# A two-layer graph network on one core: GpSimd copies ahead of each indirect DMA, a rebuilt placing stage, and fp32 query and value tables

## The chip, the core and the metric

The kernel runs on one core of a Trainium2 chip. A core has TensorE (PE, with its weight loads PEld), VectorE (DVE), ScalarE (ACT), GpSimd (POOL), a sync engine (SP) that issues plain DMAs, on-chip SBUF and PSUM, and 16 DMA engines. The metric is device time in microseconds (us) of one execution. Each engine works through its own queue in order; semaphores tie the queues together.

## What is computed

There are N = 6250 nodes with 128 features (NW = 49 windows of up to 128 rows), and E = 100000 edges, each with a source and a destination, sorted by destination in the input. Cut to what matters:

```python
# layer 0: attention over edges, H = 8 heads of D = 16
q = (x @ Wq.T + bq).reshape(N, H, D);  k, v alike
scores = sum(q[src] * k[dst], -1) / sqrt(D) + mask          # E x H
weights = softmax of scores over the edges of one src
out = segment_sum(v[src] * weights, dst) ; x = layernorm(x + out @ Wo.T + bo)
# layer 1: edge network
h = silu(concat(x[src], x[dst], attr) @ eW1 + eb1)
e = silu(h @ eW2 + eb2) ; agg = segment_sum(e, src)
x = layernorm(x + silu(concat(x, agg) @ nW1 + nb1) @ nW2 + nb2)
```

## The kernel before

The kernel is written with a queue for each engine and hand-placed semaphores; nothing reorders it. Its stages follow one another with a barrier between them. Edges are handled in tiles of 128, one edge a partition. The edges are first sorted by source: each edge gets a slot such that a tile of 128 slots holds only edges whose sources lie in one window of 128 nodes. There are 784 input tiles and 832 slot tiles (NT). Four stages issue indirect DMAs from GpSimd, one DMA for a tile of 128 rows, so 128 indices each:

- **Placing** (`place_and_project`), 98 groups of PG = 8 tiles. For each group DVE writes one-hots of the node in the window (`place_oh`) and of the window (`place_ohw`), PE transposes the first (`turn`, L588), forms which edges of a tile share a node (`gram`, L596), keeps a running table of the next free slot (`count`, L607 brings the old table into PSUM as fp32, L610 adds the counts, 400 down to 50 columns), and reads each edge's slot out (`slots_of`, L622 in fp32 and L623 in bf16). ACT copies the table (L541) and two copies of the transpose (L549, L550). DVE masks, reduces and turns the slot into a row number (`finish`, L483 to L521) and copies the 8 tiles' records into `rec_out` (L519). POOL then issues 8 indirect DMAs that scatter 64-byte records to DRAM (`send`, L646). In every second group PE also projects one window of x to q, k, v (L580 bias, L581 product). ACT copies q and v out, and DVE splits each into three bf16 parts (L470, L475) and stores these in the tables `tab` and `value_tab` (L480, L481).
- **Scores** (`score`), 104 groups of SG = 8 tiles. POOL gathers 512-byte rows of k by destination (L751); the index tile `sc_idx` is written by DVE (L761) three groups ahead. PE transposes one-hots (L843) and picks query rows with three bf16 products a tile, one for each part of the table (L853). DVE multiplies (L779) and reduces.
- **Weighing** (`weigh`), 208 groups of 4 tiles: values picked in three bf16 products (L1202), weighted, edges of one destination merged in a tile (L1212), and scattered with an add into one of four sums in DRAM (L1060). Every one of these DMAs has a semaphore wait and increment of its own ahead of it (L1058, L1059).
- **Edge network** (`edges`), 208 groups of 4 tiles: POOL gathers 512-byte rows (L1685) with indices that DVE writes (L1694); PE does transposes, `inputs` (L1790 to L1795), `second` (L1806) and `sums` (L1816); ACT turns and applies silu (L1749, L1755, L1760); DVE makes one-hots, widens them (L1707) and adds sums (L1716).

The gathers have a ring of RING = 4 buffers. In the score stage the queue of GpSimd holds, for a group, one wait on the index and one on the buffer, then 8 DMAs with nothing between them; in the edge network 4 DMAs. `c.tab` holds 3 x NP bf16 values a partition, where NP = 6272.

## Time and profile before

| what | value |
|---|---|
| median of 3 runs | 6206.48 us (6205.77 to 6213.38) |
| profiled execution: its own time | 6212.46 us |
| its span, first to last instruction | 6210.7 us |
| busy share of the span: PE, POOL, DVE, ACT | 64%, 59%, 36%, 18% |
| DMA moved | 238.36 MB, 38 GB/s on average |
| mean granted TensorE clock | 0.709 of 2.4 GHz |

How to read it. The share of an engine over the whole span hides the stages: each has its own limit. A group row of the profile gives the busy time of all its instructions, the mean duration of one, and the idle time just ahead of them, with what ended it: a named instruction (a semaphore that it posted), "issue" (nothing that the profile shows), or "remote" (the engine was released by a semaphore for which the profile finds no post at that moment). A timeline row gives start and duration in us of one instruction or of several merged ones (xN).

### The profile page before, as it was taken

The numbers are of one execution on the slowest core, as the hardware profiler recorded it, in microseconds if no ns is written. First come the engines' busy times: TensorE is split into PE (matmuls) and PEld (weight loads), VectorE is DVE, ScalarE is ACT, GpSimd is POOL, SyncE is SP. The second block draws the span as 40 slices with busy tenths as digits, with TensorE's granted clock in tenths as the row PEclk, the third lists the DMA queues.
The fourth block names the chain that finished last, engine by engine and source line by source line (L and its number), as shares of the span: only waits on it lengthen the run. The fifth ranks groups of instructions, "written<-read, shape, count | busy, mean of one in ns | idle before, by whom it ended". The sixth has DMA issues, their size and how long they took to land. (4 is left out here: it accounts for less than half of the span.)

```text
span 6210.7 us, 91570 instructions
## 1 busy us (share of the span) xinstructions
PE 3972.2 (64%) x25409; PEld 3165.9 (51%) x25410; DVE 2244.2 (36%) x6257; ACT 1098.0 (18%) x1914; POOL 3674.3 (59%) x3321
## 2 busy tenths in 40 slices
PE   6899999994333443430666666666445887777786
PEld 4556656663222222220555555555424777777774
DVE  6334444442222222329333333333244333333333
ACT  0222222220101111110111111111111222222222
POOL 0465555555666666650888888888702565555551
PEclk9996555555555565565777777777657888888888
DMA  2100000001111111110443434443341111111111
GB/s 102 68 10 10 10 9 10 10 10 62 42 44 44 42 43 43 42 40 0 36 36 35 35 35 35 35 35 35 33 126 40 40 42 40 41 40 41 41 40 53
DMA packets 278673, 238.36 MB, mean 38 GB/s; under 512 B 57254, under 2 KB 246758, under 8 KB 278245
## 3 DMA queue, kind: packets, MB, share of 16 engines
q0 software_dynamic: 198144, 170.19, 17.7%
q1 hardware_dynamic: 77604, 54.50, 2.8%
q10 hardware_dynamic: 2880, 13.11, 0.5%
q8 instruction: 24, 0.39, 0.0%
q14 instruction: 21, 0.17, 0.0%
HBM read 143.89 MB, written 93.71 MB: 38 GB/s over the span
## 5 line engine op out<-in xcount | busy, mean ns | idle before, releaser
L1060 POOL DMA_INDIRECT sums_dram<-we_merged_rows,we_idx x832 | 1287.0, 1547 | 425.7 <-issue 200.7
L1685 POOL DMA_INDIRECT ed_bg<-b_rows_dram,ed_idx x832 | 801.2, 963 | 550.6 <-issue 246.3
L652 POOL DMA_INDIRECT records_dram<-rec_out,row_idx x784 | 769.0, 981 | 568.1 <-DVE rec_out L519 331.4
L751 POOL DMA_INDIRECT sc_k<-k_rows_dram,sc_idx x832 | 800.5, 962 | 463.5 <-issue 250.3
L1212 PE MATMUL ps_merged<-we_rows,we_same_dst 128*128 128x129 f32 x1664 | 357.0, 381 | 584.7 <-issue 435.7
L853 PE MATMUL ps_q<-tab,sc_oht 128*128 x2496 | 366.6, 261 | 403.7 <-issue 398.5
L1212 PEld LDWEIGHTS ps_merged<-we_rows,we_same_dst 128*128 128x128 f32 x1664 | 305.6, 274 | 619.3 <-issue 609.3
L1816 PE MATMUL ps_ed_s<-ed_ohf,ed_efs 128*128 128x128 f32 x1664 | 427.4, 413 | 178.5 <-ACT ed_efs L1760 140.7
L853 PEld LDWEIGHTS ps_q<-tab,sc_oht 128*128 128x128 bf16 x2496 | 248.8, 104 | 522.8 <-issue 469.3
L779 DVE TENSOR_TENSOR sc_prods<-ps_q,sc_k 128x1024 f32<-128x1024 f32 x104 | 127.2, 1223 | 915.2 <-remote 862.5
L1816 PEld LDWEIGHTS ps_ed_s<-ed_ohf,ed_efs 128*128 128x128 f32 x1664 | 336.5, 227 | 222.8 <-issue 183.7
L1113 DVE SCALAR_TENSOR_TENSOR we_firsts<-we_merged_rows,lane_unmark,two_marks 128x4 f32<-128x4 f32 x208 | 46.3, 222 | 1014.8 <-ACT we_merged_rows L1156 1014.8
L622 PE MATMUL ps_slots<-place_table,place_oh_tf 128*128 128x50 f32 x1568 | 408.4, 410 | 0.0
L459 DVE TENSOR_TENSOR place_earlier<-ps_gram,tri 128x512 bf16<-128x512 f32 x196 | 126.2, 686 | 763.0 <-PE ps_gram L596 414.4
L622 PEld LDWEIGHTS ps_slots<-place_table,place_oh_tf 128*128 128x128 f32 x1568 | 401.3, 330 | 0.6 <-issue 0.6
L1191 PE MATMUL ps_dst_row<-ident,we_dsts 128*128 128x128 f32 x1664 | 352.8, 384 | 0.0
L1707 DVE CAST ed_ohf<-ed_oh 128x512 f32<-128x512 bf16 x208 | 93.1, 448 | 717.2 <-PE ps_ed_s L1816 443.6
L1156 ACT ACTIVATE we_merged_rows<-ps_merged 128x516 f32<-128x516 f32 x208 | 125.0, 601 | 1280.9 <-DMA sums_dram<-we_merged_rows,we_idx 1266.8
L843 PE MATMUL ps_oht<-identb,sc_oh 128*128 128x128 bf16 x832 | 101.7, 283 | 371.6 <-ACT sc_oht L816 203.3
L1191 PEld LDWEIGHTS ps_dst_row<-ident,we_dsts 128*128 128x128 f32 x1664 | 337.7, 300 | 0.0
L610 PE MATMUL ps_table<-place_ohw,place_oh 128*128 128x400 bf16 (+7 forms) x784 | 332.4, 581 | 0.0
L1792 PE MATMUL ps_z<-ed_oht,tab 128*128 128x128 bf16 x2496 | 302.8, 226 | 40.6 <-issue 39.0
(286 smaller groups left out, 7575.2 us busy)
## 6 DMA issues: line engine op xcount, KB each, us to landing
sc_k<-k_rows_dram,sc_idx POOLq DMA_INDIRECT x832
sums_dram<-we_merged_rows,we_idx POOLq DMA_INDIRECT x832
ed_bg<-b_rows_dram,ed_idx POOLq DMA_INDIRECT x832
sums_dram<-zero_rows ACTq DMA_DIRECT2D x20, 640.0 KB, 8.5
records_dram<-rec_out,row_idx POOLq DMA_INDIRECT x784
co_rows<-sums_dram SPq DMA_DIRECT2D x48, 256.0 KB, 3.9
records_dram<-rfill SPq DMA_DIRECT2D x16, 416.0 KB, 6.9
records<-records_dram SPq DMA_DIRECT2D x1, 6656.0 KB, 18.6
```

The costliest lines, as they stand in the source:

```text
L610: ins = pe.matmul(table[:, k + 1:PG + 1, :], ohl[:, b, :, k], ohw[:, b, :, k].unsqueeze(1).to_broadcast([P, PG - k, WC]), start=False, sto ...
L622: pe.matmul(slots[b][:, k, :], ltf[:, b, k, :], kept[:, b, k, :], start=True, stop=False)
L652: pool.indirect_dma_start(c.rec_rows, bass.IndirectOffsetOnAxis(ap=idx[:, b, j:j + 1], axis=0), out[:, b, j, :], None, bounds_check=SLOTS ...
L751: pool.indirect_dma_start(kg[:, r, k * F:(k + 1) * F], None, c.k_dram[:, :], bass.IndirectOffsetOnAxis(ap=idx[:, r, k:k + 1], axis=0)).the ...
L779: dve.tensor_tensor(prod[:, :], psq[r % 2][:, :], kg[:, r, :], ALU.mult).then_inc(s_prod, 1)
L853: ins = pe.matmul(psq[b][:, k * F:(k + 1) * F], oht[:, b, k, :], c.tab[:, j, bass.ds(win[k] * F, F)], start=(j == 0), stop=(j == 2))
L1060: pool.indirect_dma_start(c.acc_dram[k][:, :], bass.IndirectOffsetOnAxis(ap=idx[:, r, k:k + 1], axis=0), rows[:, r, k, 0:F], None, compute ...
L1191: ins = pe.matmul(psd[:, k * P:(k + 1) * P], dst[:, r, k:k + 1].to_broadcast([P, P]), c.ident[:, :], start=True, stop=True)
L1212: ins = pe.matmul(merged[b][:, k, 0:F + 1], same[:, b, k, :], con[:, b, k, :], start=True, stop=True)
L1685: pool.indirect_dma_start(bg[:, r, k * F:(k + 1) * F], None, c.b_dram[:, :], bass.IndirectOffsetOnAxis(ap=idx[:, r, k:k + 1], axis=0)).the ...
L1792: pe.matmul(z, c.tab[:, j, bass.ds(win[k] * F, F)], oht[:, b, k, :], start=False, stop=False)
L1816: ins = pe.matmul(pss[b][:, k * P:(k + 1) * P], ef[:, b, k, :], ohf[:, b, :, k], start=True, stop=True)
```

## The change

- **Copies ahead of each DMA.** In the score stage and in the edge network GpSimd itself now writes the index tile, by one copy of a 128x1 column a tile (`index`), for the group ahead, one copy in front of each gather. Each gather has a wait on the count of these copies and a semaphore increment of its own. DVE's index casts (L761, L1694) are gone. In placing, GpSimd copies each tile's 128x16 record into `rec_out`, one copy ahead of its DMA, where DVE copied 8 tiles at once (L519). The scatter of the weighing stage is as before.
- **Placing rebuilt.** The one-hot of the window is laid out tile by tile (contiguous in the product), the old table is added by DVE (`keep`, which also splits the new table in two bf16 parts) and no longer by PE and ACT, `slots_of` is three bf16 products a tile, and ACT copies the transpose once. The window's one-hot is written inside `finish`. PE's order in a step is now count, gram, slots. The bias product is bf16, with three parts of the bias in three rows.
- **Tables in fp32.** ACT writes q and v straight into two fp32 tables; the parts and their splitting on DVE are gone. In scores and weighing a tile takes one fp32 product where it took three bf16 ones.

```diff
+def blocks_onehot(dve, c, e, t0, out):
+    return dve.tensor_tensor(out, c.iotab[:, 0:WC, 0].unsqueeze(1).to_broadcast([P, PG, WC]),
+                             e.hi[:, bass.ds(t0, PG)].unsqueeze(2).to_broadcast([P, PG, WC]), ALU.is_equal)
...
+                def keep(i, b):
+                    g = 2 * i + b
                     wait_count(dve, s_slots, g - 1)
+                    dve.wait_ge(s_hist, g + 1)
+                    wait_count(dve, s_tab, 2 * g)
+                    before = e.start[:, :] if isinstance(g, int) and g == 0 else kept[:, 1 - b, PG, :]
+                    dve.tensor_copy(kept[:, b, 0, :], before).then_inc(s_tab, 1)
+                    dve.tensor_tensor(kept[:, b, 1:PG + 1, :], pstab[:, 0:PG * WC].rearrange("p (k w) -> p k w", w=WC),
+                                      before.unsqueeze(1).to_broadcast([P, PG, WC]), ALU.add).then_inc(s_tab, 1)
+                    dve.wait_ge(s_tab, 2 * g + 2)
+                    dve.tensor_copy(kb[:, b, 0], kept[:, b, 0:PG, :]).then_inc(s_parts, 1)
+                    dve.wait_ge(s_parts, 2 * g + 1)
+                    dve.tensor_tensor(kb[:, b, 1], kept[:, b, 0:PG, :], kb[:, b, 0], ALU.subtract).then_inc(s_parts, 1)
...
-                    for by, work in ((1, earlier), (2, nodes), (0, finish), (2, windows)):
+                    for by, work in ((2, nodes), (1, keep), (1, earlier), (0, finish)):
...
-                    act.activation(lt[:, :, :].rearrange("p k n -> p (k n)"), pst[:, :], ACT.Copy).then_inc(s_lt, 1)
-                    act.activation(ltf[:, b].rearrange("p k n -> p (k n)"), pst[:, :], ACT.Copy).then_inc(s_lt, 1)
+                    act.activation(lt[:, b].rearrange("p k n -> p (k n)"), pst[:, :], ACT.Copy).then_inc(s_lt, 1)
...
+                    cols = bass.ds(win * F, F)
+                    act.activation(c.qtab[:, cols], psx[:, 0:F], ACT.Copy, scale=0.25)
+                    act.activation(c.vtab[:, cols], psx[:, 2 * F:3 * F], ACT.Copy).then_inc(s_qv, 1)
...
-                    pe.matmul(psx[:, 0:3 * F], one[:, :], bias[:, :], start=True, stop=False)
+                    pe.matmul(psx[:, 0:3 * F], c.ones[:, :], bk[:, :], start=True, stop=False)
...
-                        pe.matmul(slots[b][:, k, :], ltf[:, b, k, :], kept[:, b, k, :], start=True, stop=False)
-                        ins = pe.matmul(slots[b][:, k, :], gm[:, b, k, :], ohw[:, b, :, k], start=False, stop=True)
+                        for j in range(2):
+                            pe.matmul(slots[b][:, k, :], lt[:, b, k, :], kb[:, b, j, k, :], start=(j == 0), stop=False)
+                        ins = pe.matmul(slots[b][:, k, :], gm[:, b, k, :], ohw[:, b, k, :], start=False, stop=True)
...
+                def record(g, b, j):
+                    pool.tensor_copy(out[:, b, j, :], e.rec[:, bass.ds(g * PG + j, 1), :].rearrange("p t r -> p (t r)")
+                                     ).then_inc(s_rec, 1)
 
                 def send(i, b):
                     g = 2 * i + b
-                    pool.wait_ge(s_rec, g + 1)
+                    wait_count(pool, s_sent[b], 16 * PG * i)
+                    record(g, b, 0)
                     pool.wait_ge(s_idx, g + 1)
-                    pool.sem_inc(s_turn, 1)
                     for j in range(PG):
+                        if j + 1 < PG:
+                            record(g, b, j + 1)
+                        pool.wait_ge(s_rec, PG * g + j + 1)
+                        pool.sem_inc(s_turn, 1)
                         pool.indirect_dma_start(
...
+                def index(g, r, k):
+                    pool.tensor_copy(idx[:, r, k:k + 1], c.rec[:, bass.ds(g * SG + k, 1), C_DST]).then_inc(s_idx, 1)
+
                 def gather(g, r):
-                    pool.wait_ge(s_idx, g + 1)
                     wait_count(pool, s_prod, g - RING + 1)
-                    pool.sem_inc(s_turn, 1)
+                    ahead, slot, there = group_at(g, r, 1, NS)
+                    if there:
+                        wait_count(pool, s_k[slot], (ahead - slot) * (16 * SG // RING))
                     for k in range(SG):
+                        if there:
+                            index(ahead, slot, k)
+                        pool.wait_ge(s_idx, SG * g + k + 1)
+                        pool.sem_inc(s_turn, 1)
                         pool.indirect_dma_start(kg[:, r, k * F:(k + 1) * F], None, c.k_dram[:, :],
...
-                        for j in range(3):
-                            ins = pe.matmul(psq[b][:, k * F:(k + 1) * F], oht[:, b, k, :],
-                                            c.tab[:, j, bass.ds(win[k] * F, F)], start=(j == 0), stop=(j == 2))
+                        ins = pe.matmul(psq[b][:, k * F:(k + 1) * F], oht[:, b, k, :],
+                                        c.qtab[:, bass.ds(win[k] * F, F)], start=True, stop=True)
```

The gather of the edge network is changed as the one of the score stage, with G = 4 in the place of SG, and the value product of the weighing stage as the query product.

How the queues move. First POOL in the loop of the score stage (`sc_k` is the ring of gathered rows, `sc_index`, `sc_prod` and `sc_k_in1` are semaphores; ISA and REGISTER_ALU rows are address and count arithmetic). Before:

```order
L88 REGISTER_ALU [waits sc_index]
L751 DMA sc_k<-k_rows_dram,sc_idx 128x128 [waits sc_prod]
L751 DMA sc_k<-k_rows_dram,sc_idx 128x128 x7
L747 REGISTER_ALU
L88 REGISTER_ALU [waits sc_index]
```

and after:

```order
L88 REGISTER_ALU [waits sc_prod]
L750 ISA [waits sc_k_in1]
L750 COPY sc_idx<-records 128x1
L760 ISA
L762 DMA sc_k<-k_rows_dram,sc_idx 128x128 [waits sc_index]
L750 ISA
L750 COPY sc_idx<-records 128x1
```

Eight DMAs in a row have become eight pairs of a copy and a DMA, and the wait on DVE's index has become one on POOL's own copies.

Then POOL in the loop of placing. Before:

```order
L239 ISA
L652 DMA records_dram<-rec_out,row_idx 106496x16 [waits rec_slot,row_index]
L652 DMA records_dram<-rec_out,row_idx 106496x16 x7
L648 REGISTER_ALU
L652 DMA records_dram<-rec_out,row_idx 106496x16 [waits rec_slot,row_index]
```

and after:

```order
L642 ISA [waits records_sent1]
L642 COPY rec_out<-records 128x16
L649 REGISTER_ALU
L642 ISA [waits row_index]
L642 COPY rec_out<-records 128x16
L655 DMA records_dram<-rec_out,row_idx 106496x16 [waits rec_slot]
```

The wait on DVE's copy of the records (`rec_slot`) is now one on POOL's own, and only the row index still comes from DVE.

Last, PE in placing (`ps_table` is the running table of slots, `place_oh_tf` and `place_oh_t` the fp32 and bf16 transposes). Before:

```order
L623 MATMUL ps_slots<-place_ohw,place_earlier 128x50
L622 MATMUL ps_slots<-place_table,place_oh_tf 128x50
L623 MATMUL ps_slots<-place_ohw,place_earlier 128x50
L607 MATMUL ps_table<-place_table,ident 128x450 [waits place_table_kept,place_onehot_w]
L610 MATMUL ps_table<-place_ohw,place_oh 128x400
```

and after:

```order
L606 MATMUL ps_table<-place_ohw,place_oh 128x100
L606 MATMUL ps_table<-place_ohw,place_oh 128x50
L595 MATMUL ps_gram<-place_oh_t 128x128 [waits place_earlier,place_onehot_t]
L595 MATMUL ps_gram<-place_oh_t 128x128 x7
L618 MATMUL ps_slots<-place_table_parts,place_oh_t 128x50 [waits masked,place_parts,place_earlier]
L618 MATMUL ps_slots<-place_table_parts,place_oh_t 128x50
L619 MATMUL ps_slots<-place_ohw,place_earlier 128x50
```

The 450-column fp32 product is gone, the fp32 product of each tile has become two bf16 ones, and slots now stand behind count and gram.

## Rows read from the trace of the kernel before

**Rows 1.** Busy time of each engine in the four stretches with indirect DMAs.
```profile
core 0: us, PE busy (x) PEld busy (x) DVE busy (x) ACT busy (x) POOL busy (x), PEclk, DMA share, GB/s
190.00:1481.00 1291.00, 1174.12 (x4999) 769.58 (x4998) 526.65 (x1695) 266.42 (x431) 768.56 (x784) 0.63 0.05 10
1513.00:2776.00 1263.00, 488.13 (x3401) 341.91 (x3401) 342.10 (x609) 136.36 (x249) 800.44 (x832) 0.59 0.18 43
2948.00:4489.00 1541.00, 927.08 (x6630) 883.36 (x6630) 500.94 (x1742) 232.92 (x461) 1286.95 (x832) 0.74 0.40 35
4751.00:6093.00 1342.00, 1062.18 (x8555) 949.40 (x8554) 439.51 (x1627) 359.24 (x614) 800.86 (x832) 0.86 0.17 41
```

**Rows 2.** Groups of GpSimd instructions: busy us, mean ns | idle us before, releasers.
```profile
L1060 POOL DMA_INDIRECT sums_dram<-we_merged_rows,we_idx x832 | 1287.0, 1547 | 425.7 <-issue 200.7 <-DVE we_idx L1126 176.8 <-DMA sums_dram<-we_merged_rows,we_idx 47.6
L1685 POOL DMA_INDIRECT ed_bg<-b_rows_dram,ed_idx x832 | 801.2, 963 | 550.6 <-issue 246.3 <-remote 195.3 <-PE ps_z L1795 78.6
L751 POOL DMA_INDIRECT sc_k<-k_rows_dram,sc_idx x832 | 800.5, 962 | 463.5 <-issue 250.3 <-DVE sc_idx L761 213.2
L652 POOL DMA_INDIRECT records_dram<-rec_out,row_idx x784 | 769.0, 981 | 568.1 <-DVE rec_out L519 331.4 <-issue 236.7
```

**Rows 3.** Timeline of GpSimd in the score stage: start, duration, [idle before].
```profile
2013.19 0.94 POOL L751 DMA_INDIRECT sc_k<-k_rows_dram,sc_idx  x1 [0.30 <-issue]
2014.44 0.95 POOL L751 DMA_INDIRECT sc_k<-k_rows_dram,sc_idx  x1 [0.30 <-issue]
2022.75 0.95 POOL L751 DMA_INDIRECT sc_k<-k_rows_dram,sc_idx  x1 [7.36 <-DVE sc_idx L761]
```

**Rows 4.** Timeline of PE and ACT in the score stage, up to the same pause.
```profile
1980.01 3.16 PE L853 MATMUL ps_q<-tab,sc_oht 128*128 x24
1983.17 0.68 PE L843 MATMUL ps_oht<-identb,sc_oh 128*128 128x128 bf16 x8
...
1993.72 0.27 PE L853 MATMUL ps_q<-tab,sc_oht 128*128 x1 [1.13 <-issue]
...
2019.67 1.02 ACT L816 ACTIVATE sc_oht<-ps_oht 128x1024 bf16<-128x1024 bf16 x1 [38.55 <-remote]
```

**Rows 5.** Timeline in the edge network around one pause of GpSimd.
```profile
5220.86 0.94 POOL L1685 DMA_INDIRECT ed_bg<-b_rows_dram,ed_idx  x1 [0.30 <-issue]
5221.97 0.60 ACT L1760 ACTIVATE ed_efs<-ps_ed_o 128x512 f32<-128x512 f32 x1 [8.52 <-remote]
...
5224.38 0.94 POOL L1685 DMA_INDIRECT ed_bg<-b_rows_dram,ed_idx  x1 [2.57 <-remote]
```

**Rows 6.** Waits (us, times, longest): score stage, edge network (two), weighing stage.
```profile
DVE sc_prods L779 <- remote: 862.5, 60, 29.4
...
ACT ed_efs L1760 <- remote: 352.2, 43, 10.1
ACT ed_hts L1755 <- remote: 312.8, 90, 11.5
...
ACT we_merged_rows L1156 <- DMA sums_dram<-we_merged_rows,we_idx: 1266.8, 202, 6.9
```

**Rows 7.** Timeline of GpSimd in the weighing stage.
```profile
3602.14 1.54 POOL L1060 DMA_INDIRECT sums_dram<-we_merged_rows,we_idx  x1 [0.30 <-issue]
```

**Rows 8.** Timeline of placing: GpSimd's pause and PE in one group.
```profile
814.72 0.97 POOL L652 DMA_INDIRECT records_dram<-rec_out,row_idx  x1 [4.50 <-DVE rec_out L519]
815.43 1.83 PE L607 MATMUL ps_table<-place_table,ident 128*128 128x450 f32 x2
...
817.05 3.39 PE L610 MATMUL ps_table<-place_ohw,place_oh 128*128 128x400 bf16 x8
...
820.26 1.03 PE L596 MATMUL ps_gram<-place_oh_t 128*128 128x128 bf16 x8
```

**Rows 9.** Small GpSimd instructions at the program's start: timeline.
```profile
0.35 0.10 POOL L1987 MEMSET const-float32-1.0<- 128x1 f32 x1
0.39 0.10 POOL L1987 MEMSET const-bfloat16-1.0<- 128x1 bf16 x1
...
1.93 0.19 POOL L122 CAST lane_float<-lane_int 128x1 f32<-128x1 int32 x1
```

**Rows 10.** Timeline of the edge network: unstrided fp32 products, four tiles.
```profile
5204.19 1.05 PE L1806 MATMUL ps_ed_o<-w,ed_hts 128*128 128x128 f32 x8
```

160 lines of the change are left out of this document (70 added, 90 removed).

## The prediction

> **What bounds the kernel now.** I read the busy times of four stretches first, then GpSimd's groups, then timelines. The four stages with indirect DMAs fill 5437 of the 6210.7 us [rows 1]; what lies between them (softmax, collecting, normalising) is untouched. For each stage the question is what sets the pace of a DMA.
>
> Placing takes 1291 us for 784 DMAs, 1.65 us each. PE is busy for 1174.12 us of it, POOL for 768.56 [rows 1]. POOL pauses between groups, and what ends the pause is DVE's record copy [rows 8], 331.4 us in total [rows 2]. So placing is bound by PE, and by DVE behind it.
>
> The score stage takes 1263 us for 832 gathers, 1.52 us each. PE is busy for 39%, DVE for 27%, POOL for 63% [rows 1]. A gather is 0.95 us and the next starts 0.30 us later [rows 3], so GpSimd alone would need 832 x 1.25 = 1040 us. The rest is 213.2 us of waiting for DVE's index [rows 2]. But DVE is not busy then. It waits 862.5 us for "remote" [rows 6]. The timelines show something odd: after a run of gathers PE, which did 24 products in 3.16 us, gives out single products with idle gaps of over a microsecond and no wait in them, and ACT's copy of transposes that PE finished by 1983.9 starts at 2019.67 [rows 4]. That is after the gather of 2014.44 was over and GpSimd had nothing more to issue [rows 3]. The edge network has it too: a gather ends at 5221.80, and ACT's silu, after 8.52 us of "remote", starts at 5221.97 [rows 5]. ACT sits 665 us behind "remote" there [rows 6] and GpSimd itself 195.3 us [rows 2]. I read this so: while GpSimd issues gathers back to back, semaphores and instructions of the others come late; when it pauses they catch up, and it pauses only because their lateness reaches it. The edge network takes 1342 us, 6.45 us a group, where PE has 1062.18 / 208 = 5.1 us of work and GpSimd 4 x 1.25 = 5.0.
>
> The weighing stage is the contrast. GpSimd's DMAs stand 0.30 us apart there too, at 1.54 us each [rows 7], but each has a wait of its own ahead of it. ACT's idle time there is put down to landing DMAs, 1266.8 us [rows 6], which is real dependence. This stage is bound by GpSimd.
>
> **The change part by part.** Call c what a copy adds to the period of a DMA. All three stages then hang on it, since I expect each to be bound by GpSimd.
>
> *The copy.* No row shows a copy beside an indirect DMA. From below: two memsets of one column start 0.04 us apart [rows 9], so c is at least about 0.05. From above: a one-column cast takes 0.19 us [rows 9], and if the 0.30 us of handing over [rows 3] were paid a second time, c would be 0.49. The handing over stands ahead of DMAs; small instructions show none of that size between them. I take the cast's duration, c = 0.19.
>
> *Score stage.* The index no longer comes from DVE; the wait on the buffer (`sc_prod`) asks for a product one group older than the old index did, and the wait on the ring's old gathers is long met. If the copies let the others run, the stage is 832 x (1.25 + 0.19) = 1198 us, 65 less. One fp32 product replaces three bf16 ones: 1.05 / 4 = 0.26 us a tile [rows 10] against 3.16 / 8 = 0.40 [rows 4], from different clocks; even at double the first, 0.52, a group's PE work would be some 6 us of the 11.5 that GpSimd takes. Nothing gained or lost.
>
> *Edge network.* GpSimd needs 4 x 1.44 = 5.76 us a group against PE's 5.1, so 832 x 1.44 = 1198 us, 144 less than 1342. PE would be 89% busy and each lateness would show; I add 10 us.
>
> *Placing, PE.* The 450-column fp32 product goes (1.83 us [rows 8], 1.6 of it on PE's path). The counts cost at most the 3.39 us of now [rows 8], less if contiguous one-hots read faster. Slots are 24 bf16 products; at the 1.03 / 8 = 0.13 us of the gram [rows 8] they take 3.1. With gram and turn at 1.0 to 1.1 each and half a projection at 1.2 (its bias product in one pass), the sum is at most 9.8 us a group.
>
> *Placing, DVE.* It is busy for 526.65 / 98 = 5.4 us a group [rows 1]. The splitting and the record copy leave, about 1.2; `keep` comes, four instructions of up to 400 columns, at most 2.5. That gives at most 6.7 us, and the two engines overlap, since PE counts and makes slots for one group while DVE finishes another. What is late next is GpSimd: 8 x (1.28 + 0.19) = 11.8 us. Its period of 1.28 is 0.981 of duration [rows 2] and 0.30 of gap. Placing: 784 x 1.47 = 1151 us, 140 less. The bias parts (eight instructions of 384 columns on DVE ahead of the first projection) cost 5 us once.
>
> *Weighing.* Its scatters are unchanged, and PE has 614 us of slack [rows 1] for the fp32 value product. Nothing.
>
> *The sum.* -140 - 65 - 144 + 15 = -334 us. The profiled span becomes 5877 us. The profiled execution took 6212.46 us, 1.8 over its span and 6.0 over the median, so the median becomes 5877 + 1.8 - 6.0 = about **5875 us**. The gain is gone at c = 0.19 + 334 / 2448 = 0.33 us.
>
> **A rule that speaks against it.** In these stages DVE is busy for 1308 of 3896 us, 34% [rows 1]. The gathers of now hardly feel it: their mean is 962 ns [rows 2] and single ones take 940 to 950 [rows 3].
> The Trainium skill (SBUF — State Buffer, "Who interferes with whom" and the port rules ahead of it) says that VectorE and GpSimd share a pair of ports as an exclusive lock, for VectorE's fast modes and, against a GpSimd instruction that reads SBUF, for those with two SBUF inputs. By that rule the copies, which move from DVE's queue to GpSimd's, would now queue behind DVE; by the rows on the gathers the lock costs little.
>
> **The rivals.**
> *The others stay starved* (the change does not do what it seems made for). The pauses then remain and the copies come on top. For it: a wait every four DMAs in the edge network does not help now, and the weighing stage differs from the gathers in more than its waits, being slower and of the other direction. Against it: in the edge network the release comes 0.17 us after GpSimd falls still [rows 5], so a short stretch without descriptors may be enough. Price: +158 in the score stage, +158 in the edge network, -140 in placing, together +176, about 6380 us. It decides if copies open no gap for the others.
> *The handing over is paid twice*, c = 0.49: 1388 + 1448 + 1448 = 4284 against 3896, so about 6590 us, slower. It decides from c = 0.33. For it: every DMA in the trace has 0.30 ahead of it. Against it: that gap is no longer in the weighing stage, where two more queue entries stand between DMAs [rows 7].
> *The copy is nearly free*, c = 0.05: placing 1041, scores 1082, and the edge network then at PE's pace, some 5.3 us a group or 1102. That is 671 less, with the 15 added about 5550 us. For it: the memsets, and the chance that the copy hides in the 0.30.
> *Copies held up by DVE*: a third of them meeting a DVE instruction and waiting half of some 0.4 us gives 2448 x 0.34 x 0.2 = 166 us, about 6040 us. The skill's rule on the shared ports is the mechanism.
>
> **How the numbers follow.** The forecast with c between 0.10 and 0.28 has 0.46 (5650 to 6090 by itself), the nearly free copy 0.16, DVE's hold-up 0.07, starvation that stays 0.18, the double handing over 0.13. About 0.2% is what a measurement of this kernel can tell from no change. Faster by more: 0.46 + 0.16 + 0.07 less 0.02 for the edge of the forecast, 0.67; slower 0.13 + 0.18 less 0.01, 0.30; within it 0.03. The range leaves out the double handing over and less than half of the free copy: 5560 to 6430 us.
>
> **What would show it.** Right: GpSimd's copies near 0.19 us, DMAs 1.44 to 1.47 us apart without long pauses in all three stages, "remote" waits of ACT and DVE mostly gone, placing's PE well under 80% busy. Starvation stays: "remote" again in hundreds of us and pauses of 5 us and more in the score stage. Double handing over: 0.30 us both ahead of and behind each copy. Wrong in another way: placing still with pauses that a row index of DVE ends, which would make the rebuilt chain through `keep` the bound.

## The result, and the profile after

The changed kernel took 6101.7 us (6088.9 to 6106.9, 4 runs) against 6209.2 us (6205.8 to 6213.4, 4 runs) of the kernel before, measured together: a ratio of 0.983, 95% interval 0.981 to 0.984. That is 108 us less, where 334 less was forecast. Its profiled execution has a span of 6095.8 us.

Busy time of each engine in the four stretches of the changed kernel, as in [rows 1]:

```profile
core 0: us, PE busy (x) PEld busy (x) DVE busy (x) ACT busy (x) POOL busy (x), PEclk, DMA share, GB/s
183.00:1353.00 1170.00, 499.75 (x4755) 384.63 (x4752) 624.72 (x1637) 126.22 (x239) 962.63 (x1566) 0.59 0.05 11
1386.00:2632.00 1246.00, 441.13 (x2572) 379.18 (x2572) 337.04 (x509) 137.73 (x253) 980.70 (x1655) 0.60 0.16 44
2801.00:4341.00 1540.00, 920.82 (x5810) 879.26 (x5810) 499.55 (x1742) 232.92 (x461) 1286.18 (x832) 0.79 0.39 35
4604.00:5981.00 1377.00, 1096.88 (x8589) 967.57 (x8590) 421.30 (x1435) 364.88 (x614) 991.18 (x1660) 0.85 0.15 40
```

Placing fell from 1291 to 1170 us, and PE is busy for 43% of it, no longer 91%. The score stage fell by 17 us only, the weighing not at all, and the edge network grew by 35 us.

GpSimd's groups, to set beside [rows 2] (busy us, mean ns | idle us before, releasers):

```profile
L1701 POOL DMA_INDIRECT ed_bg<-b_rows_dram,ed_idx x832 | 808.3, 972 | 196.7 <-issue 119.9 <-POOL ed_idx L1689 76.9
L762 POOL DMA_INDIRECT sc_k<-k_rows_dram,sc_idx x832 | 804.2, 967 | 152.5 <-issue 132.4 <-POOL sc_idx L750 20.0
L655 POOL DMA_INDIRECT records_dram<-rec_out,row_idx x784 | 776.5, 990 | 206.4 <-issue 108.2 <-POOL rec_out L642 98.2
L642 POOL COPY rec_out<-records 128x16 f32 (+1 forms) x784 | 190.2, 253 | 151.1 <-POOLq L289 112.2 <-DVE row_idx L508 38.2
L1689 POOL CAST ed_idx<-records 128x1 int32 (+1 forms) x832 | 184.8, 222 | 188.4 <-PE ps_z L1809 101.8 <-remote 84.5
L750 POOL CAST sc_idx<-records 128x1 int32 (+1 forms) x832 | 179.7, 217 | 112.4 <-DVE sc_prods L789 109.1
```

In the score stage and the edge network GpSimd no longer waits for an index of DVE. It waits instead for the buffer that DVE's product (`sc_prods`) or PE's product (`ps_z`) frees: 112 us in the score stage and 188 us in the edge network, of which 84.5 are put down to remote. The longest of these pauses in the score stage is 5.8 us. Its timeline in the score stage, beside [rows 3]:

```profile
1998.17 0.96 POOL L762 DMA_INDIRECT sc_k<-k_rows_dram,sc_idx  x1 [0.16 <-issue]
1999.14 0.19 POOL L750 CAST sc_idx<-records 128x1 int32 x1
1999.49 0.96 POOL L762 DMA_INDIRECT sc_k<-k_rows_dram,sc_idx  x1 [0.16 <-issue]
```

A gather starts 1.32 us after the one before, where it was 1.25: the copy takes 0.19 us, but of the 0.30 us of handing over only 0.16 is left behind it. What PE does meanwhile, beside [rows 4]:

```profile
2022.61 0.37 PE L862 MATMUL ps_q<-tab,sc_oht 128*128 x1 [1.73 <-issue]
2024.71 0.37 PE L862 MATMUL ps_q<-tab,sc_oht 128*128 x1 [1.73 <-issue]
2026.81 0.37 PE L862 MATMUL ps_q<-tab,sc_oht 128*128 x1 [1.73 <-issue]
```

The single products with idle time ahead and no wait in them are still there, here 2.10 us apart. In the score stages of both kernels such products start about 0.7, 1.4, 2.1 or 2.8 us apart, most often 0.7, 1.4 or 2.1, though GpSimd's gathers start 1.25 us apart in one and 1.32 in the other. The remote waits are still there too, beside [rows 6]; the one in placing (`place_oh_t`) is new:

```profile
DVE sc_prods L789 <- remote: 821.2, 49, 32.4
...
ACT place_oh_t L552 <- remote: 558.9, 59, 18.4
...
ACT ed_efs L1774 <- remote: 348.1, 55, 10.2
```

Waits of this size need not cost anything: placing has 558.9 us of them on ScalarE, and GpSimd, which sets its pace, has one wait for another engine in it, of 38.2 us (the L642 row above).

One thing has to be known before the experiments are read. Kernels measured together ran on one chip, one after the other; I call that a job. In some jobs the others' work comes late as above, and in other jobs never. I call them late and prompt. Within a job the times of one kernel agree to a fraction of a per cent, so a job is one or the other. The measurement that the prediction was about was a late job.

### The profile page after: what moved, and what is told of

It is laid out like the page before. It is cut to its first block and busy times, and to the rows that moved or that the text cites. A ratio compares the mean times of both kernels' runs of the same rounds, so it can differ in the third digit from the quotient of the medians.

```text
span 6095.8 us, 90649 instructions
## 1 busy us (share of the span) xinstructions
PE 3277.9 (54%) x23500; PEld 2834.4 (46%) x23501; DVE 2316.0 (38%) x5904; ACT 960.4 (16%) x1718; POOL 4241.2 (70%) x5768
## 5 line engine op out<-in xcount | busy, mean ns | idle before, releaser
L1220 PE MATMUL ps_merged<-we_rows,we_same_dst 128*128 128x129 f32 x1664 | 335.4, 364 | 589.9 <-issue 436.7
L1220 PEld LDWEIGHTS ps_merged<-we_rows,we_same_dst 128*128 128x128 f32 x1664 | 286.5, 259 | 625.4 <-issue 616.1
L862 PE MATMUL ps_q<-tab,sc_oht 128*128 x1664 | 341.5, 358 | 219.9 <-issue 206.0
L862 PEld LDWEIGHTS ps_q<-tab,sc_oht 128*128 128x128 f32 x1664 | 294.8, 260 | 249.2 <-issue 248.9
L853 PEld LDWEIGHTS ps_oht<-identb,sc_oh 128*128 128x128 bf16 x832 | 79.8, 159 | 672.7 <-issue 515.2
L606 PE MATMUL ps_table<-place_ohw,place_oh 128*128 128x400 bf16 (+7 forms) x784 | 161.7, 382 | 379.9 <-DVE place_ohw L229 217.4
L1200 PE MATMUL ps_dst_row<-ident,we_dsts 128*128 128x128 f32 x1664 | 328.2, 364 | 0.0
L1689 POOL CAST ed_idx<-records 128x1 int32 (+1 forms) x832 | 184.8, 222 | 188.4 <-PE ps_z L1809 101.8
L606 PEld LDWEIGHTS ps_table<-place_ohw,place_oh 128*128 128x128 bf16 x784 | 111.4, 162 | 436.0 <-issue 378.3
L1200 PEld LDWEIGHTS ps_dst_row<-ident,we_dsts 128*128 128x128 f32 x1664 | 314.0, 281 | 0.0
```

What stands on the lines that cost most here:

```text
L606: ins = pe.matmul(table[:, k:PG, :], ohl[:, b, :, k], ohw[:, b, k, :].unsqueeze(1).to_broadcast([P, PG - k, WC]), start=(k == 0), stop=Tru ...
L853: ins = pe.transpose(pst[:, k * P:(k + 1) * P], oh[:, r % 2, :, k], c.identb[:, :])
L862: ins = pe.matmul(psq[b][:, k * F:(k + 1) * F], oht[:, b, k, :], c.qtab[:, bass.ds(win[k] * F, F)], start=True, stop=True)
L1200: ins = pe.matmul(psd[:, k * P:(k + 1) * P], dst[:, r, k:k + 1].to_broadcast([P, P]), c.ident[:, :], start=True, stop=True)
L1220: ins = pe.matmul(merged[b][:, k, 0:F + 1], same[:, b, k, :], con[:, b, k, :], start=True, stop=True)
L1689: pool.tensor_copy(idx[:, r, k:k + 1], c.rec[:, bass.ds(g * G + k, 1), C_DST]).then_inc(s_idx, 1)
```

## The experiments

Stage times below are from the first to the last start of the stage's indirect DMAs, and a period is the median distance of two starts.

### Parts of the change, one by one

Index copies back to VectorE (placing and tables stay changed):

```diff
+                    pool.wait_ge(s_idx, g + 1)
...
-                        if there:
-                            index(ahead, slot, k)
-                        pool.wait_ge(s_idx, SG * g + k + 1)
```

> The changed kernel, but in the two gathers the index copies are VectorE's again, one for a group, as in the kernel before; placing keeps its GpSimd copies, queries and values their fp32 tables. Theory A: a copy lengthens a gather's period by the 0.064 to 0.071 us that the changed kernel shows, and takes away only part of the pauses, because these come from the others being served late while GpSimd issues gathers back to back; so score returns to about 1263 us (+18) and the edge network to about 1342 us (-34), and the whole is about 6086 us, within 0.5% of the changed kernel. Theory B: the copies are what held the pauses down, and what the changed kernel gained in the score stage is theirs; then score and edge network both grow, by 70 us together or more, 6170 us or more.

Measured: 5572.5 us, but the kernel before took 5702.7 us beside it, not 6209; ratio 0.977 (0.975 to 0.979). Both theories had priced it for a kernel before of 6209 us, so neither could be judged from the absolute time. This job was prompt. The two gather stages took 1048 and 1057 us.

The records of placing by VectorE too:

```diff
+                    dve.tensor_copy(out[:, b, :, :], e.rec[:, bass.ds(g * PG, PG), :]).then_inc(s_rec, 1)
...
-                            record(g, b, j + 1)
```

> As the run before, and the records of placing are copied by VectorE too, one copy for a group of 8 (behind the row index): GpSimd issues DMAs alone, as in the kernel before, but placing keeps its rebuilt counting and slots and its lighter TensorE. Theory A: a placing that GpSimd paces at 1.28 us a scatter takes 784 x 1.28 = 1003 us, plus what it waits for VectorE; if the others are starved there as in the score stage of the kernel before (222 us of pauses in 832 gathers), it takes some 1200 us. So placing lies between 1003 and 1210 us against 1169 us; theory A says pauses ended by VectorE's records or row index of 100 to 200 us in all, and the whole between 6000 and 6120 us. Rival (the shared port): the 115 us that the copies cost beyond 0.067 each in placing come from VectorE and GpSimd holding each other up; without copies placing then falls under 1070 us and the whole under 5990 us.

Measured: 5464.2 us, 0.958 (0.957 to 0.960). Placing is 1060 us, against 1164 us with the eight GpSimd copies. That lies in theory A's range and under the rival's 1070 us as well, and both had reckoned with a late job, so it does not decide between them.

The kernel before with the index copies alone:

> The kernel before with one part of the change alone: GpSimd copies the index in front of each gather, in the score stage and the edge network. Placing, tables and products are those of before. Theory A (starving has nothing to do with how many products TensorE has to fetch): score as in the changed kernel, 1245 us (-17 against before), edge network 1376 us (+34), the whole about 6226 us, +0.3%. Rival (TensorE's 24 products a group in place of 8 are what comes late): score stays at or above 1263 + 54 = 1317 us, since each period grows by 0.064 and no pause goes; the whole 6270 to 6300 us.

Measured: 5838.7 us, 1.024 (1.022 to 1.026). So where nothing comes late, the index copies by themselves cost 136 us, 0.08 us for each of 1664: the stages took 1132 and 1119 us. They take nothing away, since there were no pauses to take away.

A slower gather, by a memset of 128x512 that waits for its own end, in front of each:

> The changed kernel with a memset of 128x512 fp32 (its result used by nobody) on GpSimd in front of each gather of the score stage and the edge network: the gathers start some 1.85 us apart, as the scatters of the weighing do, instead of 1.32. Theory P (the pace of the DMAs starves the others): waits for a remote releaser on VectorE, ScalarE and TensorE in these stages fall from hundreds of us to under 60 us each, GpSimd has no pause over 1 us, score and edge network take 832 x 1.85 = 1540 us each; the whole about 6560 us. Theory K (the kind of DMA, a gather, starves them at any pace): the waits and the pauses stay (150 us in score, 275 us in the edge network), and the whole is 6900 us or more.

Measured: 7552.7 us. The gathers started 2.42 us apart, not 1.85, because 0.81 us of idle time stood behind the memset:

```profile
1999.54 0.53 POOL L762 MEMSET sc_slow<- 128x512 f32 x1
2000.87 0.97 POOL L766 DMA_INDIRECT sc_k<-k_rows_dram,sc_idx  x1 [0.81 <-issue]
```

The job was prompt, so there was no lateness that a slower pace could have taken away; the run is inconclusive.

### Both kernels again, and two versions without copies

> The kernel before, unchanged, for a trace from the chip on which the experiments run. In the four runs so far no wait was put down to a remote releaser and the kernel before took 5703 us there, against 6209 us where the change was measured. Theory C (the late serving of the other engines is a property of the chip on which the kernel was profiled, not of GpSimd's pace): the trace has no remote waits over 30 us, score takes 832 x 1.263 = 1050 us without pauses (it was 1263), the edge network about 1070 us (it was 1342), placing still about 1290 us, held by TensorE. Rival (it comes and goes with the run): remote waits are back in hundreds of us and the whole is near 6209 us.

Measured: 5702.5 us, and not one wait of the trace is put down to remote. GpSimd's groups in it, beside [rows 2]:

```profile
L1685 POOL DMA_INDIRECT ed_bg<-b_rows_dram,ed_idx x832 | 805.4, 968 | 262.6 <-issue 233.4 <-DVE ed_idx L1694 25.0 <-PE ps_z L1795 4.3
L751 POOL DMA_INDIRECT sc_k<-k_rows_dram,sc_idx x832 | 798.9, 960 | 254.3 <-issue 253.2 <-DVE sc_idx L761 1.1
L652 POOL DMA_INDIRECT records_dram<-rec_out,row_idx x784 | 767.4, 979 | 571.1 <-DVE rec_out L519 350.2 <-issue 221.0
```

The wait for DVE's index is 1.1 us where it was 213.2, the `remote` of the edge network is gone, and the record copy's wait in placing is as it was. PE hands out its 24 products in one go here, in the middle of a run of gathers:

```profile
1999.98 3.25 PE L853 MATMUL ps_q<-tab,sc_oht 128*128 x24
```

The edge network's row, beside [rows 1], has a granted TensorE clock of 0.99 of 2.4 GHz where it was 0.86, and PE busy for 96% of the stage:

```profile
4535.00:5594.00 1059.00, 1011.82 (x8669) 901.80 (x8667) 443.07 (x1641) 371.20 (x621) 805.36 (x832) 0.99 0.21 52
```

The transfers themselves are not slower in a late job. The queue of GpSimd's DMAs moved the same packets in about the same time: 17.7% of 6210.7 us, or 1099 us, in the late trace of this kernel, and 19.4% of 5700.8, or 1106 us, in the prompt one (packets, MB, share of the span of 16 engines):

```profile
q0 software_dynamic: 198144, 170.19, 17.7%
...
q0 software_dynamic: 198144, 170.19, 19.4%
```

> The changed kernel, unchanged, on the chip of the experiments. Theory C, where no wait is remote: its gathers have copies that cost 136 us in all (the kernel before with these copies alone was that much slower than without them), and the kernel without the copies took 5573 us; so 5573 + 136 = 5709 us, a ratio of 1.001 to the kernel before: no change. Rival (the gain is the kernel's everywhere): 0.983 x 5703 = 5605 us. Where this chip turns out to be like the first one, both kernels give 6102 and 6209 us again.

Measured: 5700.3 us, 10 runs, ratio 0.9999 (0.9989 to 1.0008). **Where nothing comes late, the change is worth nothing**: placing -129 us, score stage +77, edge network +61, and 6 us less between the stages.

```profile
L762 POOL DMA_INDIRECT sc_k<-k_rows_dram,sc_idx x832 | 825.2, 992 | 131.3 <-POOL sc_idx L750 117.9 <-issue 8.7 <-DVE sc_prods L789 4.8
L1701 POOL DMA_INDIRECT ed_bg<-b_rows_dram,ed_idx x832 | 807.3, 970 | 131.5 <-POOL ed_idx L1689 127.0 <-issue 4.5
```

Records copied by ScalarE, which is idle for most of placing; indices by VectorE:

```diff
+                def records(i, b):
+                    g = 2 * i + b
+                    wait_count(act, s_sent[b], 16 * PG * i)
+                    act.activation(out[:, b, :, :], e.rec[:, bass.ds(g * PG, PG), :], ACT.Copy).then_inc(s_rec, 1)
```

> As the run without any GpSimd copies (5464 us against 5703 us), but ScalarE, not VectorE, copies the records of placing (one copy of 128x128 fp32 a group of 8); indices of the gathers by VectorE. There GpSimd paused 165 us for the records behind VectorE's row index, and this goes: 5464 - 165 = 5300 us if nothing else is late, and 5400 to 5464 us if VectorE's row index, which waits for the scatters' landing in its two buffers, takes the place of it.

Measured: 5451.6 us, 0.957 (0.955 to 0.958), at the dear end of what was expected. Placing is 1046 us, 14 less than with VectorE's copy. My 165 us were misread. In e2's timeline 151 of them stand ahead of the stage's first scatter, and only 14 lie between groups:

```profile
183.16 1.22 POOL L648 DMA_INDIRECT records_dram<-rec_out,row_idx  x1 [151.19 <-DVE rec_out L510]
```

The index of a whole group in one GpSimd copy:

```diff
-                    pool.tensor_copy(idx[:, r, k:k + 1], c.rec[:, bass.ds(g * SG + k, 1), C_DST]).then_inc(s_idx, 1)
+                    pool.tensor_copy(idx[:, r, :], c.rec[:, bass.ds(g * SG, SG), C_DST]).then_inc(s_idx, 1)
```

> As the run with ScalarE's record copies, but the index copies of the gathers are on GpSimd, one for a whole group (8 columns in the score stage, 4 in the edge network) in place of one a gather. It costs 104 + 208 copies of about 0.2 us, at most 62 us, and takes away the waits for VectorE's index (24 us where no wait is remote, over 200 us where the kernel was first profiled). So where no wait is remote: 0 to +40 us against the run before it; where remote waits are back: 150 us less or more.

Measured: 5505.0 us, 0.966 (0.964 to 0.967), 53 us more than without it: a little over the 0 to 40 expected. The score stage took 1087 us, the edge network 1083 us.

> The version without any GpSimd copies (records by ScalarE, indices by VectorE) once more, on whatever chip the job comes to; the kernel before runs beside it. Theory C (the remote waits belong to single chips): either the kernel before takes 5700 us, no wait of this kernel is remote and it takes 5450 us, or the kernel before takes some 6200 us, remote waits of hundreds of us are back, and this kernel lies between 5900 and 6100 us, since the placing it shortens (by 245 us) is then starved as the other two stages are. Rival (remote waits come with chance in single runs): any mixture of the two.

Measured: 5457.6 us, 0.957, on a third chip; no remote waits, the kernel before 5705 us. At this point my theory C ("single chips are late") looked good.

### A late job, and the pace

> The kernel before with the fp32 tables alone: ScalarE writes queries and values once in fp32, VectorE no longer splits them, score and weighing have one product a tile; placing is not rebuilt and there are no GpSimd copies. The prediction's reading (TensorE, 88% busy, bounds the old placing, GpSimd the rest): placing stays within 20 us of 1293 us, score within 5 us of 1051 us, the weighing at 1538 us, the whole at 5680 to 5705 us against 5701 us. Rival (VectorE's splitting, which stands ahead of the record copy, holds the scatters): placing falls to 1200 us or less, the whole to 5610 us or less, and most of what the rebuilt placing gives is this.

Measured: 6190.1 us against 6209.1 us, 0.998 (0.996 to 0.999). The job ran on the very chip on which the runs e5 to e8 had been prompt. **So theory C fell**: being late comes with the job and not with the chip. As to its own question: placing took 1301 us, so VectorE's splitting did not hold it, as the prediction had it; the score stage took 1231 us against 1262 us, the edge network 1338 against 1341.

Two index copies in front of each gather, the second into a buffer nobody reads:

```diff
+                    pool.tensor_copy(twice[:, r, k:k + 1], c.rec[:, bass.ds(g * SG + k, 1), C_DST]).then_inc(s_idx, 1)
...
+                        pool.wait_ge(s_idx, 2 * (SG * g + k + 1))
```

> The changed kernel with a second index copy of one column behind the first in front of each gather (into a buffer that nobody reads). Where no wait is remote the first copy costs 0.096 us a gather in the score stage and 0.075 in the edge network (1128 against 1048 us, 1119 against 1057 us). Theory H (the first copy is half hidden in the 0.30 us of handing over that stands between two DMAs in any case): the second has nothing to hide in and costs its 0.19 to 0.21 us, 1664 x 0.20 = 333 us, the whole about 6030 us. Rival (copies are cheap, and what the first costs is the longer DMA behind it): the second costs 0.08 or less, the whole 5830 us or less.

Measured: 6021.9 us, 0.970 (0.968 to 0.971) in this late job. **It does more work and is faster than the changed kernel**, which had 0.983 in another late job. In this very job the version with one copy ahead of each gather (e12, next) took 1249 and 1380 us in the two stages; two copies took 1232 and 1321. That the 6022 us lie near theory H's 6030 is chance: theory H had priced a prompt job. The timeline and the groups of GpSimd:

```profile
2001.12 0.97 POOL L764 DMA_INDIRECT sc_k<-k_rows_dram,sc_idx  x1 [0.15 <-issue]
2002.10 0.19 POOL L751 CAST sc_idx<-records 128x1 int32 x1
2002.22 0.18 POOL L752 CAST sc_twice<-records 128x1 int32 x1
2002.56 0.97 POOL L764 DMA_INDIRECT sc_k<-k_rows_dram,sc_idx  x1 [0.15 <-issue]
```

```profile
L751 POOL CAST sc_idx<-records 128x1 int32 (+1 forms) x832 | 202.8, 244 | 2.8
```

The gathers start 1.44 us apart, and GpSimd's wait for the score stage's buffer is gone: 2.8 us ahead of the index copy, where the changed kernel has 112.4. No wait of DVE's product is put down to remote. But the version of this job without any index copies (e10) took 1231 and 1338 us: against none, two copies gain 17 us in the edge network and nothing in the score stage. One copy is the worst of the three in both.

One record copy a group of 8 tiles on GpSimd, in placing:

> The changed kernel, but in placing GpSimd copies the records of 8 tiles at once (128x128 fp32) in place of 8 copies of 128x16; the gathers keep their copies. Theory N (what the copies cost there goes with their number: 784 of them, with scatters 1.345 us apart instead of 1.277, and another 110 us of longer periods): placing is 784 x 1.277 = 1001 us and 98 copies of some 0.4 us in the open, 1040 to 1070 us against 1164 us, the whole 5580 to 5610 us against 5700 us. Rival (GpSimd's copies and VectorE hold each other up, by the amount copied and not by the number): placing stays within 25 us of 1164 us.

Measured: 6150.8 us, 0.990 (0.988 to 0.993), late. Placing took 1220 us, longer than with eight copies (1167 us in e11, in the same job), neither theory's 1040 to 1070 nor within 25 us of 1164: fewer copies let the scatters start at 1.28 us again, and 188 us of pauses came with that.

### The rest of both kinds of job

> The version without GpSimd copies (records by ScalarE, indices by VectorE) again. The last job showed that remote waits come and go with the job and not with the chip: on one and the same chip the kernel before took 5701 us in one job and 6209 us in another. If this job is one without remote waits: 5450 us, 0.957. If it is one with them (the kernel before near 6209 us): placing, which GpSimd paces at 1.28 us a scatter without pauses, is starved too, 1046 + 150 to 250 us, score 1230 to 1262 us, edge network 1340 us, and the whole 5960 to 6080 us, 0.96 to 0.98.

Measured: 6212.2 us against 6244.8 us, 0.995 (0.993 to 0.997), in a late job. The version that gains 4.3% in a prompt job gains 0.5% in a late one. Placing grew from 1046 to 1302 us, 6 us over the 1296 at most expected, with the row index late; the score stage took 1250 us, within its range, and the edge network 1359, where 1340 was expected. The whole is above my range because I had added it up too low: 5452 + 250 + 214 + 283 would have been 6199 us. GpSimd's group in placing:

```profile
L654 POOL DMA_INDIRECT records_dram<-rec_out,row_idx x784 | 803.1, 1024 | 651.5 <-issue 388.4 <-DVE row_idx L508 224.2 <-ACT rec_out L557 38.9
```

The weighing's scatters write in place of adding:

```diff
-                                                rows[:, r, k, 0:F], None, compute_op=ALU.add).then_inc(s_sent[k], 16)
+                                                rows[:, r, k, 0:F], None).then_inc(s_sent[k], 16)
```

> The changed kernel, but the scatters of the weighing write their rows in place of adding them, so its sums are left out of the output. Such a scatter should take GpSimd about 1 us like the scatter of placing, and the weighing's DMAs start 1.28 us apart, until the others (VectorE, TensorE) bound it. In a job without remote waits: weighing 832 x 1.28 = 1065 us or what VectorE allows. In a job with them: theory P (pace) says that remote waits now appear in the weighing, where there were none at 1.85 us, in hundreds of us, on VectorE or ScalarE; theory K (it is the gathers, the kind of DMA) says that none appear, and the weighing takes the same as in a job without them.

Measured: 6083.3 us, late. A scatter takes 0.96 us now, the period is 1.27 us, and remote waits appear in a stage whose trace of before has none. The weighing took 1442 us. The first row has one wait of 173.0 us ahead of the first scatter, and the third is the real dependence, 1266.8 us before [rows 6]:

```profile
POOL sums_dram L1069 <- DVE we_idx L1135: 480.3, 65, 173.0
ACT we_merged_rows L1165 <- remote: 366.7, 60, 9.7
...
ACT we_merged_rows L1165 <- DMA sums_dram<-we_merged_rows,we_idx: 310.3, 77, 7.0
```

> The version with a second index copy in front of each gather once more, since the first time was in a job with remote waits, where it made the gathers start 1.43 us apart, took away nearly all pauses of the score stage and was 80 us faster than the version with one copy. In a job without remote waits there is nothing to relieve: the second copy costs 1664 x 0.12 (the growth of the median period) = 200 us, score 1128 + 100, edge network 1119 + 100, the whole 5900 us, slower than the kernel before by 3.5%. In a job with them: 6022 us again.

Measured: 6117.2 us, 0.979 (0.977 to 0.981). The job was late, so it repeated the finding (against 0.970), and its question stayed for the next one. The stages took 1235 and 1367 us, where one copy took 1253 and 1404 us in the same job (e14).

> The version with two index copies a gather, for a job without remote waits, which its two jobs so far were not. There: score 832 x 1.434 = 1193 us against 1128 us with one copy, edge network 832 x 1.442 = 1200 us against 1119 us, the whole 5700 + 146 = 5846 us, 2.5% slower than the kernel before. If the job has remote waits: 0.970 to 0.979 of the kernel before again.

Measured: 5897.6 us, 1.034 (1.032 to 1.036), in a prompt job: the same kernel that gains 2 to 3% in a late job loses 3.4%. The stages took 1233 and 1211 us. The forecast of 5846 us was 52 too low, because it took each stage as 832 median periods; the 5900 us of e15, from the growth of the stages, was right. The second copy costs 0.12 us a gather: the two casts of 0.19 us start only 0.12 us apart (above), and the stages grew by 105 and 92 us, 0.13 and 0.11 us a gather. So theory H of e11, 0.20 us, is wrong, and so is its rival of 0.08.

> The version with one GpSimd copy of 8 tiles' records in placing, for a job without remote waits (its first job had them, and its placing took 1220 us, with 188 us of pauses). Theory N (the cost goes with the number of copies between DMAs): placing 1040 to 1070 us against 1164 us, the whole 5580 to 5610 us, 0.98 of the kernel before. Rival: 1140 us or more. If the job has remote waits: 0.990 again.

Measured: 5652.8 us, 0.991 (0.990 to 0.993), prompt. Placing took 1117 us, two fifths of the way from 1164 to 1046: over the 1070 of theory N and under the rival's 1140. It misses theory N since the copy has a DMA behind it only 1.15 us after the one ahead of it ended:

```profile
810.07 0.97 POOL L652 DMA_INDIRECT records_dram<-rec_out,row_idx  x1 [0.30 <-issue]
811.04 0.31 POOL L642 COPY rec_out<-records 128x128 f32 x1
812.19 0.97 POOL L652 DMA_INDIRECT records_dram<-rec_out,row_idx  x1 [0.84 <-issue]
```

That is 0.85 us more than the 0.30 of two scatters, 83 us for 98 groups.

> The version whose weighing writes in place of adding, once more, for a job without remote waits (its first had them: weighing 1442 us at a median period of 1.27 us, 366.7 us of remote waits on ScalarE's merged rows). Theory P: without remote waits GpSimd runs at 1.27 us without pauses and the weighing takes 832 x 1.27 = 1055 us, or up to 1200 us where VectorE, busy for 510 us, and TensorE, busy for 881 us, hold it by themselves. Rival: 1400 us or more, so the pauses of the first job were VectorE's and TensorE's own pace and had nothing to do with remote waits. In a job with remote waits: 1442 us again.

Measured: 5218.2 us, prompt. The weighing took 1055 us, GpSimd's own pace (832 x 1.263 = 1051 us):

```profile
L1069 POOL DMA_INDIRECT sums_dram<-we_merged_rows,we_idx x832 | 798.3, 960 | 425.1 <-DMA sums_dram<-we_merged_rows,we_idx 241.3 <-DVE we_idx L1135 169.5 <-issue 13.4
```

The same kernel took 1442 us in the late job, so its pauses there were not VectorE's and TensorE's own pace. Each of the two jobs has one run of it.

### What the runs show together

| stage and version | period, us | prompt, us | late, us | cost of lateness |
|---|---|---|---|---|
| weighing, scatters that add | 1.85 | 1538 | 1539 | 0 |
| score, two copies | 1.43 | 1233 | 1232, 1235 | 0 |
| score, one copy (the change) | 1.32 | 1128, 1129 | 1244 to 1253 | 115 to 125 |
| score, no copy | 1.25 | 1048 to 1055 | 1231 to 1262 | 176 to 214 |
| edges, two copies | 1.44 | 1211 | 1321, 1367 | 110 to 156 |
| edges, one copy (the change) | 1.32 | 1119, 1120 | 1375 to 1404 | 255 to 285 |
| edges, no copy | 1.25 | 1056 to 1059 | 1338 to 1359 | 279 to 303 |
| placing, eight copies (the change) | 1.35 | 1162 to 1165 | 1167 to 1213 | 2 to 51 |
| placing, one GpSimd copy a group | 1.28 | 1117 | 1220 | 103 |
| placing, records by ScalarE | 1.28 | 1046, 1048 | 1302 | 254, 256 |
| weighing, scatters that write | 1.27 | 1055 | 1442 | 387 |

The closer GpSimd's indirect DMAs follow each other, the more lateness costs in a late job, and scatters show it as gathers do. The waits show it as well: DVE's product in the score stage waited 862 us for "remote" at 1.25 us, 821 at 1.32 and not at all at 1.43 (ScalarE kept 133 us of such waits there in one of the two late traces, e15), and the weighing has such waits at 1.27 us only.

Two cautions. Period is not the only thing that differs between these versions: a copy is also a further instruction between two DMAs, and a scatter that writes is another kind of transfer than one that adds; in placing two versions with the same 1.28 us lose 103 and about 255 us. And the cost falls in large part because the prompt time rises: late, the score stage takes 1231 to 1262 us in all its versions. A limit that each stage has of its own in a late job, whatever GpSimd does, would look much the same. Against it speak the waits that vanish and placing, which takes 1302 us late without GpSimd copies and 1167 to 1213 us with eight. No run separates the two.

At one pace the stages do differ: the edge network still loses 110 us or more at 1.44 us, where the score stage loses nothing. PE is busy there for 1100 of 1322 us (e11), in the score stage for 490 of 1234. That this is why, is argued, not shown.

## Why the prediction was right or wrong, point by point

**The reading was right.** GpSimd back to back, the others late, the weighing bound by GpSimd, the old placing by PE and by DVE's record copy behind it. The prompt jobs confirm the arithmetic: score 832 x 1.25 = 1040 forecast as GpSimd's own need, 1051 measured, with 1.1 us of waiting for the index. What it could not see in one trace is that the lateness is a matter of the job.

**Placing: right.** -140 forecast, -122 in the late job and -129 in a prompt one. PE at 43% instead of "well under 80%", counts at 1.72 us for 8 where at most 3.39 was allowed, and slots of 24 products in 1.1 us where 3.1 was allowed:

```profile
799.70 1.72 PE L606 MATMUL ps_table<-place_ohw,place_oh 128*128 128x400 bf16 x8 [4.08 <-DVE place_ohw L229]
```

That the sum came so near is luck, though: its parts compensate. The period is 1.345 us, not 1.47, which would be 1054 us; the other 110 us, of which the forecast had none, are mostly the wait at each group's start, on GpSimd's own copy (some 85 us), and copies that run long. The GpSimd record copies cost 104 us against VectorE's single copy (1164 against 1060) and 118 against ScalarE's.

**The copy: mis-sized.** c was taken as 0.19 us, the whole duration of a cast. It is 0.064 to 0.076 us by the median period, and by the prompt stage times 0.07 us in the edge network and 0.09 in the score stage. The row on two memsets 0.04 us apart [rows 9], my lower bound, was the nearer one, because the copy's 0.19 us lies partly in the 0.30 us of handing over that was there before. In the two gather stages this error by itself made the forecast too dear, by some 0.12 x 1664 = 200 us; in placing other costs took its place.

**Score stage and edge network: the step that failed.** It is "if the copies let the others run". One copy does not: the score stage took 1246 us where 1198 was forecast (-17 for -65), and the edge network 1377 where 1208 was (+35 for -134). The runs show what stood in its place. With one copy the gathers come 1.32 us apart, and in the measured job lateness still costs 116 and 256 us. With two they come at 1.43 to 1.44 us, the period for which I had written 1198 us, and it costs 0 and 110 us or more. So the release that I counted on exists, but one copy brings little of it: the pauses stay, and each gather is dearer. A copy as dear as I thought would have brought it in the score stage, and even then not the 1198 us: two copies took 1232 and 1321 us there, late, and 1233 and 1211 prompt. In the score stage some 33 us of the rest are copies held up, of which more below. I had treated the price of the copy and its effect on the others as two independent guesses.

**The rivals.** "The others stay starved" was the right mechanism, and its signs came: remote waits in hundreds of us, and pauses of up to 5.8 us. Its price, +176 us, was too high, because it used c = 0.19 and no relief at all. "The copy is nearly free" had c nearly right (0.05) and its consequence wrong. The result lies between the two: with 0.064 and 0.071 us a gather and no relief at all, the stages would be 1316 and 1401 us, and they took 1246 and 1377. "The handing over is paid twice": no, 0.16 us stand behind the copy, and nothing ahead of it. "Copies held up by DVE": it happens, and costs less than its price. The median index copy takes 0.19 to 0.20 us, but the means are 217 and 222 ns, and in placing 253 ns where the median is 0.21, because single copies are far longer:

```profile
2000.45 0.73 POOL L750 CAST sc_idx<-records 128x1 int32 x1
2000.46 0.68 DVE L698 TENSOR_TENSOR sc_oh<-iota_by_tile,lanes 128x1024 bf16<-128x1024 bf16 x1
```

The copy ends 0.04 us after the instruction of VectorE beside it. So it is with all 231 copies over 0.3 us in this trace, of 2448: each ends within 0.06 us behind the end of a VectorE instruction, in the score stage 53 of 56 times this one, L698; of the copies under 0.22 us at most one in ten does. What they take beyond a median copy is 65 us in all, where the rival had a third of the copies held up and 166 us. That agrees with the Trainium skill (SBUF — State Buffer, "Who interferes with whom"), by which a GpSimd instruction that reads SBUF and a VectorE instruction with two SBUF inputs use a shared pair of ports that only one of them can hold, so that the other is blocked until the first is done. No run here took VectorE's instructions away.

**Tables.** Nothing was forecast, and nothing came where GpSimd sets the pace (score 1048 to 1055 us with them and 1051 without, in prompt jobs). In a late job they gave 31 us in the score stage (1231 against 1262) and 19 us in all, with fewer instructions of PE to come late. That I missed. In that same late job the stages with tables and one copy (e12) took 1249 and 1380 us, beside 1231 and 1338 with tables alone (e10): even late, the index copies cost 18 and 42 us. What made the changed kernel faster is the rebuilt placing, and a little the tables.

## What to carry to other kernels

Before building on a wait that the profile puts down to "remote", look whether it is there in another job: the same change is worth 1.7% in a late job and 0.0% in a prompt one, and the version without GpSimd copies is worth 0.5% and 4.3%. Work that GpSimd does between indirect DMAs has two prices, its own (0.07 to 0.09 us for a first small copy, 0.12 us for a second) and what the slower pace gives back to the others; they cannot be guessed apart. Where nothing comes late, leave copies off GpSimd if it sets the pace: placing took 1164 us with its eight, 1060 with VectorE's one and 1046 with ScalarE's.

## What the runs showed of the hardware that I had not expected

- In a late job's score stage TensorE gives out single products about 0.7, 1.4, 2.1 or 2.8 us apart while GpSimd issues indirect DMAs every 1.25 or 1.32 us, and waits put down to remote last up to 39 us; in the twelve traces of prompt jobs, on five chips, no wait is remote. One chip had both. The edge network's granted TensorE clock was 0.86 in the kernel before when late and 0.99 when prompt. What makes a job late stays open: no run here controls it.
- A kernel with more work can be faster: two copies in front of each gather took 6022 us where one took 6102 us, in two late jobs whose kernel before took 6209 us each.
- Of a copy of 0.19 us on GpSimd between two indirect DMAs, 0.07 us show in the period; of a second one 0.12 us. A copy that meets an instruction of VectorE can last until that one ends: 0.73 us where the median is 0.19. A copy of 128x128 with a wait behind it shows 0.85 us.
- An indirect scatter that writes takes GpSimd 0.96 us, one that adds 1.55 us. Without the addition the weighing took 483 us less in a prompt job (1055 for 1538), and 97 us less in a late one (1442 for 1539), by one run each.
